# Windowed-attention block on Trainium2: TensorE's order of work regrouped by tile form

## The chip, the cores and the metric

The kernel runs on one core of a Trainium2 chip. The metric is the device time of one execution in microseconds. A core has TensorE (matrix products, with a separate weight load ahead of each), VectorE, ScalarE, GpSimd and a queue that issues the DMAs. In the profile they are PE, PEld (the weight loads), DVE, ACT, POOL and SP. Only TensorE writes sums into the eight banks of PSUM; VectorE and ScalarE copy them out.

A word on "tile form": an instruction uses 128 or 64 (or 32) rows of TensorE's array and 128 or 64 of its columns. The profile's lines show it: `64*100` is a product with 64 rows of input and 100 output columns, which takes the 64-row x 128-column form; `103*64` takes the 128x64 form, `64*64` the 64x64 form, `128*128` the whole array. Products in disjoint tiles of one form run side by side.

## The reference

The input x is (4, 64, 128, 128). It is normalised in 32 groups of two channels. With h = that normalised x:

```
qkv  = conv3x3_depthwise(einsum("bchw,oc->bohw", h, w_qkv) + b_qkv) + b_dw   # 192 channels
q, k, v = qkv in windows of 8 x 8 pixels, 4 heads of 16 channels
attn = softmax(q @ k.T * temperature)                # 16 x 16 per window and head
out  = attn @ v
gate = gelu(v @ w_mlp.T + b_mlp)                     # over the 64 pixels of a window
y    = x + einsum("bchw,oc->bohw", out * gate, w_proj) + b_proj
```

## The kernel before, in words

Two images lie side by side in the 128 partitions (image, channel). The picture is cut into bands of 16 rows; a band of an image pair is a chunk, 16 chunks in all. A chunk has 16 column groups and is worked in four steps, a = 0 to 3, of four column groups each; `STEPS` is 64, and step i has a = i % 4. While chunk n is in its attention steps, TensorE also makes the q, k, v of chunk n + 1 as filler (`fillers`): in steps a = 0 and 1 eight units of channel mix each (`mix_channels`, the product with w_qkv over 10 x 10 patches, line 674), in steps a = 2 and 3 three units of depthwise convolution each (`depthwise`, line 709). Filler units go alternately through two work buffers of two PSUM banks (`unit_ps`). A number in `units()` gives each unit its buffer; the semaphores `full` and `free` hand it to the engine that copies it out and back (line 326 on ScalarE, line 417 on VectorE). The order of `units()` has to be the order in which TensorE issues them.

The other four banks (`rest_ps`) belong to the attention steps. Two of them are `pair_ps`: the mixed output of `apply_probs` (line 787) in columns 0 to 255 of both, the transposed v of `turn_v` in the whole first bank and the projection (line 796) in the whole second. Two are `score_ps`: scores in columns 0 to 255 (line 747) and the gate product in the rest (line 763).

A step on TensorE is: `score(i)`, fillers, `gates` (in steps a = 1 and 3, for two steps together, written one in two places), `project(i - 1)`, `turn_v(i)` (line 773, four 128 x 128 transposes), fillers, `apply_probs(i)`, fillers. The tuple `cut` says how many fillers stand where. On VectorE a step is: `mix(i - 1)` (output times gate, line 503), `scores_up` (mask, maximum, subtraction; lines 511, 516, 518), `gate_up` (adds b_mlp, line 525), `residual(i - 1)` (line 552), `divide` (sum, reciprocal, product; lines 532 to 536), `turn` (transpose of the probabilities, line 543), one depthwise copy in step a = 2, `normalise` (line 488, patches two chunks ahead) in steps 2 and 3, and in the first chunks statistics of the second image pair (`look`, line 496). ScalarE has the copies of the fillers, `exponent` (line 341), `v_up` (the copy of the transposed v, line 347), `gelu` (line 351) and the table loads (lines 351 and 356). All orders are written out by hand; each engine runs its own in order and waits on semaphores. The chunk's first scores wait until the last two depthwise copies of the chunk are done (`qkv_of`).

## Time and profile before

| | |
|---|---|
| three runs, median | 679.08 us |
| lowest, highest | 677.62, 679.31 us |
| profiled execution, from first to last instruction | 680.0 us |
| TensorE busy in it | 625.8 us, 92% |
| weight loads busy | 549.1 us, 81% |
| VectorE busy | 511.6 us, 75% |
| ScalarE busy | 482.8 us, 71% |

The profiled execution has no other time of its own than its span. Busy time of TensorE counts an instruction until its result has drained, so a busy TensorE is not one at its peak: consecutive instructions overlap, and the time that a block of work takes is read from its start to the start of the next block.

### The profile page before, as it was taken

The numbers are of one execution on the slowest core, as the hardware profiler recorded it, in microseconds if no ns is written. First come the engines' busy times: TensorE is split into PE (matmuls) and PEld (weight loads), VectorE is DVE, ScalarE is ACT, GpSimd is POOL, SyncE is SP. The second block draws the span as 40 slices with busy tenths as digits, with TensorE's granted clock in tenths as the row PEclk, the third lists the DMA queues.
The fourth block names the chain that finished last, engine by engine and source line by source line (L and its number), as shares of the span: only waits on it lengthen the run. The fifth ranks groups of instructions, "written<-read, shape, count | busy, mean of one in ns | idle before, by whom it ended". The sixth has DMA issues, their size and how long they took to land.

```text
span 680.0 us, 32438 instructions
## 1 busy us (share of the span) xinstructions
PE 625.8 (92%) x15044; PEld 549.1 (81%) x15044; DVE 511.6 (75%) x790; ACT 482.8 (71%) x631; POOL 0.3 (0%) x5
## 2 busy tenths in 40 slices
PE   3788799999999999999999999999999999999954
PEld 2687698888989898888989898888989798888843
DVE  4872688887888888786878676786868676876684
ACT  3652678787877778786877778786877778786722
POOL 0000000000000000000000000000000000000000
PEclk9997899999999999999999999999999999999975
DMA  9872115335171714132050504132150504112022
GB/s 363 263 217 72 33 50 166 110 86 208 33 232 49 234 59 149 66 102 93 8 191 5 195 4 142 60 94 106 29 173 4 198 3 152 44 50 80 4 82 44
DMA packets 29240, 72.28 MB, mean 106 GB/s; under 512 B 9801, under 2 KB 16329, under 8 KB 24233
## 3 DMA queue, kind: packets, MB, share of 16 engines
q1 hardware_dynamic: 28674, 68.57, 31.0%
q8 instruction: 118, 1.93, 1.2%
q10 hardware_dynamic: 432, 1.65, 0.7%
q14 instruction: 16, 0.13, 0.1%
HBM read 53.44 MB, written 16.78 MB: 103 GB/s over the span
## 4 chain that ended last, share of the span: by engine, by line
PE 87%; ACT 5%; DVE 3%; issue 2%; DMA 1%; ACTq 0%; DVEq 0%
PE unit_ps L709 28%; PE unit_ps L674 26%; PE rest_ps L796 10%; PE rest_ps L787 6%; PE rest_ps L763 6%; PE rest_ps L747 6%; PE rest_ps L773 4%; ACT z L326 2%; DMA patches<-in_hot 1%; ACT dw L326 1%; PE rest_ps L643 1%; PE rest_ps L674 1%; PE unit_ps L636 0%; DVE scores L511 0%; DVE scores L536 0%
## 5 line engine op out<-in xcount | busy, mean ns | idle before, releaser
L326 ACT ACTIVATE z<-unit_ps 100x768 f32<-100x768 f32 x244 | 184.9, 808 | 60.1 <-PE unit_ps L674 60.1
L674 PE MATMUL unit_ps<-consts,patches 64*100 64x192 f32 x1984 | 195.0, 336 | 8.6 <-ACT z L326 6.6
L709 PE MATMUL unit_ps<-z,dw 103*64 103x64 f32 (+2 forms) x6144 | 194.3, 224 | 3.0 <-issue 1.7
L709 PEld LDWEIGHTS unit_ps<-z,dw 103*64 103x64 f32 (+2 forms) x6144 | 185.5, 139 | 10.7 <-issue 8.6
L674 PEld LDWEIGHTS unit_ps<-consts,patches 64*100 64x100 f32 x1984 | 153.6, 164 | 25.8 <-ACT z L326 11.2
L326 ACT ACTIVATE qkv<-unit_ps 128x1024 f32<-128x1024 f32 x78 | 79.1, 1014 | 31.5 <-PE unit_ps L709 31.4
L511 DVE TENSOR_TENSOR scores<-rest_ps,consts 128x512 f32<-128x512 f32 x64 | 44.1, 689 | 51.6 <-PE rest_ps L747 51.6
L503 DVE TENSOR_TENSOR gate<-rest_ps,gate 128x512 f32<-128x512 f32 x64 | 44.1, 689 | 47.5 <-PE rest_ps L787 44.6
L796 PE MATMUL rest_ps<-gate,consts 128*128 128x256 f32 x256 | 75.1, 417 | 1.1 <-DVE gate L503 1.0
L347 ACT ACTIVATE v_t<-rest_ps 128x512 f32<-128x512 f32 x64 | 38.2, 597 | 40.5 <-PE rest_ps L773 38.9
L341 ACT ACTIVATE scores<-scores 128x512 f32<-128x512 f32 x64 | 40.4, 631 | 33.2 <-DVE scores L518 31.6
L787 PE MATMUL rest_ps<-v_t,probs_t 64*64 64x64 f32 x2048 | 45.5, 228 | 10.5 <-DVE probs_t L543 10.1
L525 DVE TENSOR_TENSOR gate<-rest_ps,consts 128x512 f32<-128x512 f32 x64 | 44.0, 687 | 14.4 <-PE rest_ps L763 14.0
L796 PEld LDWEIGHTS rest_ps<-gate,consts 128*128 128x128 f32 x256 | 44.9, 195 | 11.9 <-issue 3.5
L747 PE MATMUL rest_ps<-qkv 64*64 64x64 f32 x2048 | 45.4, 227 | 9.0 <-issue 9.0
L787 PEld LDWEIGHTS rest_ps<-v_t,probs_t 64*64 64x64 f32 x2048 | 36.7, 137 | 20.9 <-issue 18.8
L747 PEld LDWEIGHTS rest_ps<-qkv 64*64 64x64 f32 x2048 | 37.9, 138 | 18.1 <-issue 18.1
L552 DVE SCALAR_TENSOR_TENSOR staged<-rest_ps,consts,staged 128x512 f32<-128x512 f32 x64 | 46.7, 729 | 7.5 <-PE rest_ps L796 7.5
L543 DVE STREAM_TRANSPOSE probs_t<-scores 128x512 f32<-128x512 f32 x64 | 45.5, 712 | 2.2
L763 PE MATMUL rest_ps<-consts,qkv 64*64 64x64 f32 x2048 | 45.6, 228 | 1.6 <-DVE scores L511 1.6
L763 PEld LDWEIGHTS rest_ps<-consts,qkv 64*64 64x64 f32 x2048 | 36.7, 138 | 12.3 <-issue 8.2
L518 DVE TENSOR_TENSOR scores<-scores,neg_max 128x512 f32<-128x512 f32 x64 | 44.3, 692 | 2.2
(55 smaller groups left out, 530.5 us busy)
## 6 DMA issues: line engine op xcount, KB each, us to landing
staged<-in_x SPq DMA_DIRECT2D x17, 1024.0 KB, 4.9
out_y<-staged SPq DMA_DIRECT2D x15, 1024.0 KB, 5.4
T<-in_x SPq DMA_DIRECT2D x12, 1152.0 KB, 6.7
seen<-in_x SPq DMA_DIRECT2D x32, 256.0 KB, 2.9
qkv<-in_x SPq DMA_DIRECT2D x6, 1024.0 KB, 13.9
T<-in_x SPq DMA_DIRECT2D x3, 1088.0 KB, 6.7
staged<-in_x SPq DMA_DIRECT2D x2, 512.0 KB, 22.9
out_y<-staged SPq DMA_DIRECT2D x4, 256.0 KB, 3.0
```

Source lines behind the costliest of these rows:

```text
L326: return nc.scalar.activation(to, of, ACT.Copy)
L503: nc.vector.tensor_tensor(held, pair_ps[:, :, 0:BATCH * HW], held, ALU.mult).then_inc(mixed_ready, 1)
L511: nc.vector.tensor_tensor(scores[:].rearrange("p (h g) d -> p h g d", h=2), score_ps[:, :, 0:BATCH * C].rearrange("p h (g d) -> p h g d", ...
L518: nc.vector.tensor_tensor(scores[:], scores[:], neg_max[:].unsqueeze(2).to_broadcast([P, WIDE, C]), ALU.add).then_inc(shifted, 1)
L543: nc.vector.transpose(probs_t[:].rearrange("p w d -> p (w d)"), scores[:].rearrange("p w d -> p (w d)")).then_inc(probs_t_ready, 1)
L552: nc.vector.scalar_tensor_tensor(to, proj_ps.rearrange("p (r c) -> p r c", r=BAND), b_proj, to, op0=ALU.add, op1=ALU.add).then_inc(out_rea ...
L674: last = nc.tensor.matmul(to[0:NPATCH, t, b * QKV:(b + 1) * QKV], patches[image, b, g], w1[image], start=True, stop=True)
L709: last = nc.tensor.matmul(to[h * HW:(h + 1) * HW, m // 8, m % 8 * NW:(m % 8 + 1) * NW], dw[0:used, c, :], z[0:used, c, :], start=True, sto ...
L747: last = nc.tensor.matmul(score_ps[pair, h, g * C:(g + 1) * C], q[rows, pair], k[rows, pair], start=True, stop=True)
L763: last = nc.tensor.matmul(gate_ps[side(b, h), b, g * HW:(g + 1) * HW], windows(j, g)[rows, 2, b * C:(b + 1) * C], mlp[rows], start=True, s ...
L787: last = nc.tensor.matmul(pair_ps[side(b, h), b, g * HW:(g + 1) * HW], probs_t[rows, h * BATCH + g, :], v_t[rows, at], start=True, stop=True)
L796: last = nc.tensor.matmul(proj_ps[:, b * 4 * HW:(b + 1) * 4 * HW], proj[:, b * P:(b + 1) * P], gate[:, i % GATES, b].rearrange("p g (r c) ...
```

## The change

TensorE's order is put together by tile form. `turn_v` uses two 64-row halves per column group instead of one 128 x 128 transpose and writes into a work buffer, as a unit of the ring (`turns_in`): steps 0 and 1 of a chunk (a = 0 and 1) make their own turn and that of the step two later, steps 2 and 3 make none. Its copy is a `v_up` on ScalarE for step i and one on VectorE for step i + 2; the v of steps 2 and 3 waits in its own places (`v_ts`, one of them in the space of `tap_w`). The projection is two 64-column halves per bank (`project`), or in steps after a = 3 and 0 two rounds of 64 rows (`project_half`). It writes columns 256 to 511 of both `pair_ps` banks. The gates of two steps stand behind each other ahead of `apply_probs` in steps 0 and 2; the even one writes where the projection does (`proj_ps`), the odd one beside the scores. `scores` of row half h and image b go to bank h ^ b. VectorE adds b_mlp to the two gates one step later than TensorE makes them: in step 1 ahead of `scores_up` and behind `v_up`, in step 3 behind `scores_up`. In step 3, ScalarE copies depthwise 4 and 5 out between the two GELUs.

```diff
+def turns_in(i):
+    return [("turn", j) for j in (i + 2, i)] if i % BATCHES < 2 else []
 def gates_in(i):
-    return (0, 1) if i == 0 else (i + 1, i + 2) if i % 2 and i + 2 < STEPS else ()
+    return [i + 2, i + 3] if i % 2 == 0 and i + 2 < STEPS else []
...
+        def v_up(engine, copy, i):
+            unit = ("turn", i)
+            used = i if i % BATCHES == 1 else i - 2 if i % BATCHES == 0 else i - 3
+            if used > 0:
+                engine.wait_ge(mix_done, used)
+            wait_full(engine, unit)
+            copy(v_ts[i % BATCHES].rearrange("p (h x) -> p h x", h=2),
+                 work[buffer(unit)][:, :, 0:BATCH * HW]).then_inc(free[buffer(unit)], 1)
...
                 for j in now:
                     gelu(j)
                     if more and a == 3 and j == now[0]:
                         evacuate_dw(act, copy, n, 4)
-                if more and a == 3:
-                    evacuate_dw(act, copy, n, 5)
+                        evacuate_dw(act, copy, n, 5)
...
+                now = gates_in(i - 1) if i else [0, 1]
+                if now and a == 1:
+                    gate_up(now[0])
                 scores_up(i)
-                now = gates_in(i)
+                if now and a != 1:
+                    gate_up(now[0])
+                for unit in turns_in(i)[:1]:
+                    v_up(dve, copy, unit[1])
                 if now:
-                    gate_up(now[0])
-                elif i:
+                    gate_up(now[1])
+                if i:
                     residual(i - 1)
                 divide(i)
                 turn(i)
...
             def turn_v(i):
-                if i:
-                    pe.wait_ge(mixed_ready, i)
+                unit = ("turn", i)
+                to = take(unit)
                 for g in range(BATCH):
-                    last = nc.tensor.transpose(pair_ps[:, 0, g * P:(g + 1) * P], windows(i, g)[:, 2], ident)
-                last.then_inc(v_t_done, 1)
+                    for h in range(2):
+                        rows = slice(h * HW, (h + 1) * HW)
+                        last = nc.tensor.transpose(to[:, h, g * HW:(g + 1) * HW], windows(i, g)[rows, 2],
+                                                   ident[rows, rows])
+                last.then_inc(full[buffer(unit)], 1)
...
+            def wait_gated(i):
+                pe.wait_ge(mixed_ready, i + 1)
+                for j in gates_in(i)[:1]:
+                    pe.wait_ge(gate_biased, j + 1)
             def project(i):
-                pe.wait_ge(mixed_ready, i + 1)
+                wait_gated(i)
                 for b in range(2):
-                    last = nc.tensor.matmul(proj_ps[:, b * 4 * HW:(b + 1) * 4 * HW], proj[:, b * P:(b + 1) * P],
-                                            gate[:, i % GATES, b].rearrange("p g (r c) -> p r g c", c=WS),
-                                            start=True, stop=True)
+                    for t in range(2):
+                        last = nc.tensor.matmul(proj_ps[t * C:(t + 1) * C, b],
+                                                proj[:, b * P + t * C:b * P + (t + 1) * C], gated(i, slice(0, P), b),
+                                                start=True, stop=True)
                 last.then_inc(proj_done, 1)
+            def project_half(i, second):
+                if second:
+                    pe.wait_ge(half_done, i // BATCHES * 2 + (i % BATCHES == BATCHES - 1) + 1)
+                else:
+                    wait_gated(i)
+                for b in range(2):
+                    rows = slice((b ^ second) * HW, (b ^ second) * HW + HW)
+                    last = nc.tensor.matmul(proj_ps[:, b], proj[rows, b * P:(b + 1) * P], gated(i, rows, b),
+                                            start=not second, stop=bool(second))
+                last.then_inc(proj_done if second else half_done, 1)
...
             for i in range(STEPS):
+                a, units_now, turns = i % BATCHES, fillers(i), turns_in(i)
...
                 score(i)
+                if not units_now:
                     project(i - 1)
+                    fill(turns)
+                elif a < 2:
+                    if i:
+                        fill(units_now[:1])
+                        project_half(i - 1, 0)
+                        fill(units_now[1:2])
+                    fill(turns[:1])
+                    if i:
+                        project_half(i - 1, 1)
+                    fill(turns[1:])
+                    fill(units_now[2:6])
+                elif a == 2:
+                    project(i - 1)
+                    fill(units_now)
+                else:
+                    fill(units_now[:1])
+                    project(i - 1)
+                    fill(units_now[1:])
+                for j in gates_in(i):
+                    gates(j, i)
                 apply_probs(i)
+                if a < 2:
+                    fill(units_now[6:])
             project(STEPS - 1)
```

## Rows read from the trace of the kernel before

**Rows 1.** The page, busy time, share of the span and instructions of each engine.
```profile
PE 625.8 (92%) x15044; PEld 549.1 (81%) x15044; DVE 511.6 (75%) x790; ACT 482.8 (71%) x631; POOL 0.3 (0%) x5
```
**Rows 2.** The page, chain of waits: shares of the span by engine, by line.
```profile
PE 87%; ACT 5%; DVE 3%; issue 2%; DMA 1%; ACTq 0%; DVEq 0%
PE unit_ps L709 28%; PE unit_ps L674 26%; PE rest_ps L796 10%; PE rest_ps L787 6%; PE rest_ps L763 6%; PE rest_ps L747 6%; PE rest_ps L773 4%; ACT z L326 2%; DMA patches<-in_hot 1%; ACT dw L326 1%; PE rest_ps L643 1%; PE rest_ps L674 1%; PE unit_ps L636 0%; DVE scores L511 0%; DVE scores L536 0%
```
**Rows 3.** Stretches (first, fifth, last chunk): length, busy of PE, PEld, DVE, ACT, POOL, clock.
```profile
66.68:109.60 42.92, 38.59 (x974) 33.77 (x973) 32.36 (x50) 31.39 (x42) 0.00 (x0) 0.92 0.12 33
223.79:261.79 38.00, 37.14 (x929) 32.61 (x929) 32.00 (x50) 29.43 (x40) 0.00 (x0) 1.00 0.41 132
643.73:680.03 36.30, 19.77 (x356) 15.55 (x356) 24.84 (x40) 10.01 (x15) 0.00 (x0) 0.68 0.26 59
```
**Rows 4.** Timeline of PE, sixth chunk: start us, us, instructions merged [idle before <- releaser].
```profile
261.79 0.77 PE L747 MATMUL rest_ps<-qkv 64*64 64x64 f32 x32 [0.60 <-issue]
262.49 1.55 PE L674 MATMUL unit_ps<-consts,patches 64*100 64x192 f32 x16
263.97 1.13 PE L796 MATMUL rest_ps<-gate,consts 128*128 128x256 f32 x4
264.93 0.60 PE L773 MATMUL rest_ps<-consts,qkv 128*128 128x128 f32 x4
265.46 1.55 PE L674 MATMUL unit_ps<-consts,patches 64*100 64x192 f32 x16
267.27 1.60 PE L674 MATMUL unit_ps<-consts,patches 64*100 64x192 f32 x16 [0.26 <-ACT z L326]
...
273.01 0.69 PE L763 MATMUL rest_ps<-consts,qkv 64*64 64x64 f32 x32
273.63 1.13 PE L796 MATMUL rest_ps<-gate,consts 128*128 128x256 f32 x4
...
282.93 5.82 PE L709 MATMUL unit_ps<-z,dw 103*64 103x64 f32 x192
288.68 0.69 PE L787 MATMUL rest_ps<-v_t,probs_t 64*64 64x64 f32 x32
289.20 0.65 PE L747 MATMUL rest_ps<-qkv 64*64 64x64 f32 x32
289.77 2.09 PE L709 MATMUL unit_ps<-z,dw 103*64 103x64 f32 x64
...
298.57 0.69 PE L787 MATMUL rest_ps<-v_t,probs_t 64*64 64x64 f32 x32
299.87 0.69 PE L747 MATMUL rest_ps<-qkv 64*64 64x64 f32 x32 [0.60 <-issue]
```
**Rows 5.** Timeline of PE in two narrow windows: the first records of a block.
```profile
262.49 0.57 PE L674 MATMUL unit_ps<-consts,patches 64*100 64x192 f32 x4
...
263.97 0.70 PE L796 MATMUL rest_ps<-gate,consts 128*128 128x256 f32 x2
```
**Rows 6.** Timeline of ACT, sixth chunk.
```profile
263.43 1.51 ACT L326 ACTIVATE z<-unit_ps 100x768 f32<-100x768 f32 x2 [0.23 <-PE unit_ps L674]
264.83 0.63 ACT L341 ACTIVATE scores<-scores 128x512 f32<-128x512 f32 x1
265.57 0.60 ACT L347 ACTIVATE v_t<-rest_ps 128x512 f32<-128x512 f32 x1
266.41 1.51 ACT L326 ACTIVATE z<-unit_ps 100x768 f32<-100x768 f32 x2 [0.24 <-PE unit_ps L674]
...
299.79 1.28 ACT L356 ACT_TABLE_LOAD   x1
```
**Rows 7.** Timeline of DVE, sixth chunk.
```profile
287.00 1.22 DVE L417 COPY qkv<-unit_ps 128x1024 f32<-128x1024 f32 x1 [0.20 <-PE unit_ps L709]
...
289.48 0.69 DVE L503 TENSOR_TENSOR gate<-rest_ps,gate 128x512 f32<-128x512 f32 x1
...
291.52 0.69 DVE L518 TENSOR_TENSOR scores<-scores,neg_max 128x512 f32<-128x512 f32 x1
```

More of the change, by code:

```diff
@@ L66, in units @@
     for i in range(STEPS):
-        order += fillers(i)
+        fill, turns = fillers(i), turns_in(i)
+        if i == 0:
+            order += fill[:2] + turns + fill[2:]
+        else:
+            order += [*fill[:1], *fill[1:2], *turns, *fill[2:]]
     return {name: at for at, name in enumerate(order)}
@@ L236, in evacuate_dw @@
             if n > 1:
-                engine.wait_ge(v_t_done, (n - 1) * BATCHES)
+                wait_full(engine, ("turn", (n - 1) * BATCHES - 3))
             wait_full(engine, unit)
@@ L379, in _ @@
                     exponent(i)
-                    v_up(i)
+                    v_up(act, copy, i)
                     if more:
@@ L718, in fill @@
                         depthwise(*unit[1:])
+                    elif unit[0] == "turn":
+                        turn_v(unit[1])
                     elif unit[0] == "mean":
@@ L739, in score @@
                     pe.wait_ge(masked, i)
-                    pe.wait_ge(gate_biased, max(j for m in range(i) for j in gates_in(m)) + 1)
                 for g in range(BATCH):
@@ L746, in score @@
                             rows = slice(h * HW, (h + 1) * HW)
-                            last = nc.tensor.matmul(score_ps[pair, h, g * C:(g + 1) * C], q[rows, pair], k[rows, pair],
+                            last = nc.tensor.matmul(score_ps[pair, h ^ b, g * C:(g + 1) * C], q[rows, pair], k[rows, pair],
                                                     start=True, stop=True)
@@ L762, in gates @@
                             rows = slice(h * HW, (h + 1) * HW)
-                            last = nc.tensor.matmul(gate_ps[side(b, h), b, g * HW:(g + 1) * HW],
+                            last = nc.tensor.matmul(gate_ps[j % 2][side(b, h), b, g * HW:(g + 1) * HW],
                                                     windows(j, g)[rows, 2, b * C:(b + 1) * C], mlp[rows],
@@ L781, in apply_probs @@
                     pe.wait_ge(out_ready, i)
+                for j in gates_in(i)[:1]:
+                    pe.wait_ge(gate_done, j + 1)
                 for g in range(BATCH):
                     for h in range(2):
-                        at = slice((2 * g + h) * HW, (2 * g + h + 1) * HW)
+                        at = slice((h * BATCH + g) * HW, (h * BATCH + g + 1) * HW)
                         for b in range(2):
                             rows = slice(b * C, (b + 1) * C)
-                            last = nc.tensor.matmul(pair_ps[side(b, h), b, g * HW:(g + 1) * HW],
-                                                    probs_t[rows, h * BATCH + g, :], v_t[rows, at],
+                            last = nc.tensor.matmul(mix_ps[side(b, h), b, g * HW:(g + 1) * HW],
+                                                    probs_t[rows, (h ^ b) * BATCH + g, :], v_ts[i % BATCHES][rows, at],
@@ L789, in apply_probs, with gated @@
                                                     start=True, stop=True)
                 last.then_inc(mix_done, 1)
+            def gated(i, rows, b):
+                return gate[rows, i % GATES, b].rearrange("p g (r c) -> p r g c", c=WS)
+            def wait_gated(i):
+                pe.wait_ge(mixed_ready, i + 1)
+                for j in gates_in(i)[:1]:
+                    pe.wait_ge(gate_biased, j + 1)
             def project(i):
-                pe.wait_ge(mixed_ready, i + 1)
+                wait_gated(i)
```

64 lines of the change are left out of this document (23 added, 41 removed).

## The prediction

> **What bounds the kernel now.** I read the busy shares first: TensorE is busy 92% of the span, VectorE 75%, ScalarE 71% [rows 1]. The chain of waits says the same: 87% of it is TensorE, in the depthwise, channel-mix and projection products [rows 2]. The stretch view shows the repeated unit: one chunk of four steps takes 38.00 us with TensorE busy 37.14 of it [rows 3]. Fifteen such chunks make the kernel, so each 0.1 us in a chunk is 1.5 us. The last question is what TensorE's time consists of, and for that I read its order of work line by line, in the chunk behind that one [rows 4, 5].
>
> A change of tile form has a price. Two matmul blocks of the 64x64 form behind each other (apply, then scores) take 289.77 - 288.68 = 1.09 us; a lone block of it takes 273.63 - 273.01 = 0.62. So the seam costs 1.25 - 1.09 = 0.16 if the form changes and nothing if it doesn't [rows 4]. Channel mix (64 rows x 128 columns): 16 records last 1.55, 4 last 0.57, so two records take 0.163 and a unit of eight 0.65; a block of two units takes 1.48 to the next block, 0.18 over its 1.30 [rows 4, 5]. Depthwise (128x64): 3 units take 288.68 - 282.93 = 5.75; a unit is 1.87 (192 records last 5.82, 64 last 2.09, the difference over two), and 5.75 less 3 x 1.87 leaves 0.15 [rows 4]. The 128x128 block (projection and turn): 265.46 - 263.97 = 1.49, of which the projection's four records are 4 x 0.215 and the four transposes 4 x 0.109 (0.60 less one duration of 0.27, over 3); 0.19 remains [rows 4, 5].
>
> With these the four steps of a chunk before, by their tile-form blocks (5, 9, 4 and 7), are 8.48, 9.91, 8.39 and 9.88 us, together 36.66; the trace has 38.00. The 1.34 between are two waits: 0.56 where four mix units stand in a row (a pair takes 267.27 - 265.46 = 1.81 instead of 1.30, because the buffer comes free by ScalarE), and 0.79 ahead of the chunk's first scores, which wait for ScalarE's last depthwise copy (299.87 - 298.57 = 1.30 where 0.52 is work) [rows 4, 6].
>
> **The change, part by part.**
> Blocks. After, step 0 of a chunk is scores | mix, half projection, mix, turn, half, turn, 4 mix | gates, gates, apply | 2 mix. Step 1 is the same without gates. Step 2 is scores | projection, 3 depthwise | gates, gates, apply, and then step 3's scores with no seam; step 3 is 1 depthwise, projection, 2 depthwise | apply, and the next scores with no seam. That is 12 blocks instead of 25.
>
> Work inside the blocks. The projection keeps its columns: two 64-column tiles side by side, or two halves of 64 rows side by side, four rounds of 256 columns each way, 0.86. The trace has no 64-row transpose. Its lower bound is 4 rounds at a 64x64 block's pace (0.52 / 8 = 0.065), 0.26 a step; its upper bound, if the two row halves don't run side by side, is 8 x 0.109 = 0.87. I take 4 x 0.109 = 0.44, today's price: each weight load still has 128 columns, and mix shows two row halves running as a pair. The Trainium skill (TensorE: Matmul & The Clock Gate, section LDWEIGHTS) prices a load by its columns alone; an estimate by its figure would be 4 x 128 / 1.2 ns = 0.43, which no run shows yet for this form. Pure work is then step 0: 0.63 + (0.18 + 6 x 0.65 + 0.86 + 0.87) + 1.56 + 1.48 = 9.47; step 1: 0.63 + 5.81 + 0.63 + 1.48 = 8.54; step 2: 0.63 + (0.15 + 0.86 + 5.60) + 1.45 = 8.69; step 3: 0.58 + 6.61 + 0.52 = 7.71. Sum 34.41, which is 2.25 less than 36.66. (Two turns each stand in steps 0 and 1, none in 2 and 3.)
>
> New waits, the ring. The turn leaves its own bank and goes through the two work buffers, so steps 0 and 1 send ten units through the ring instead of eight. From the start of a mix unit to ScalarE's copy is 263.43 - 262.49 = 0.94, and from that copy's start to TensorE's restart in the buffer 267.27 - 266.41 = 0.86; a restarted mix unit needs 0.73, since its first weight load (0.08) isn't hidden, and a turn 0.11 more for the same reason [rows 4, 6]. I walk step 0 from the start of its scores. Mix 0 runs 0.63 to 1.36. ScalarE is not free: the second GELU (0.63, as the exponent over as many columns) now stands behind the last depthwise copy, and the table load (1.28) behind that [rows 6], so its copy of mix 0 starts at 1.9 and not at 1.57. Half projection and mix 1 end at 2.44; the first turn wants mix 0's buffer, free at 2.76, and ends at 3.30; half projection to 3.73; second turn to 4.17. VectorE copies the first turn from 3.44 to 4.13 (0.69, as for another 512 columns out of PSUM [rows 7]), so mix 2 starts at 4.19. ScalarE copies the second from 4.31 to 4.91 (0.60 [rows 6]); mix 3 starts at 4.96. Mix 4 and 5 follow 1.81 behind 2 and 3, to 7.50. Then seam and gates, gates, apply to 9.16, two mixes to 10.63: 1.16 of waits, where step 0 had 0.56. Step 1 by the same walk: the second turn waits for mix 1's copy (3.60 instead of 3.31, plus 0.11), mixes 2 to 5 start at 4.14, 4.93, 5.94, 6.74; the step takes 9.67, so 1.13 of waits where it had none. Added: 1.73.
>
> New wait, step 3. The projection there must also see gate j biased, j being the first gate of step 2, since both lie in one bank. VectorE does that behind step 2's product with the gate and step 3's three passes over the scores. From the scores' start, the product starts at 289.48 - 289.20 = 0.28 and the third pass ends at 292.21 - 289.20 = 3.01 [rows 7]; the bias add ends at 3.65, TensorE sees it at 3.7. It comes to the projection at 0.58 + 1.92 = 2.49. It waits 1.21 and restarts with 0.05: 1.26. Behind it in TensorE's queue stand two depthwise units, whose last copy holds back the next chunk's scores, so nothing gives it back. (Step 1 has the same wait, but there VectorE adds the bias ahead of the scores, and two mixes cover it.)
>
> What stays. The 0.79 ahead of the chunk's scores is unchanged: its copy still follows the last depthwise unit. In step 2 the gates wait for VectorE's copy of depthwise 1, there at 7.2 after 5.99 + 1.22 [rows 7], when TensorE comes at 7.24: 0.02. The softmax chain ends before apply in each step (7.1 against 9.1 in the tightest but one, level in step 3). The DMAs keep order and slack.
>
> Sum for a chunk: -2.25 + 1.73 + 1.26 + 0.02 = +0.76, 38.76 instead of 38.00. Fourteen chunks: +10.6. The first chunk is a case of its own (42.9 us, granted clock 0.92 on average, so partly at the lower level [rows 3]); I take it as even: two gate blocks more ahead of its first scores, and less waiting behind its first GELUs, which the longer step 0 covers in part. The last chunk is a chain VectorE - ScalarE - TensorE (36.3 us from its start to the end [rows 3]); two more 0.69 passes ahead of the softmax's end, partly in the exponent's shadow, less one moved behind, give +0.6. Together +11.2: the profiled span goes from 680.0 to 691.2, and as the median of the runs shown (679.08) lies 0.95 under that span, 690 us.
>
> A page of the Trainium skill speaks against the regrouping: PSUM, section PSUM bank collisions raise a hardware error, has it that different row tiles can't use one bank at the same time. In the scores each bank is now written from both row halves (bank h ^ b), which would make their rounds run one after the other. But the gates already write that way (both row halves into bank b, other partitions), and their block takes 0.62 to the next block [rows 4], as a scores block does; if the rule did bite, scores would take 0.47 more a step, about +28 us in all. I give it 2 in 100.
>
> **Rivals.**
> A, faster: the ring hides its waits. ScalarE is busy only 29.4 of 38 us a chunk and VectorE 32.0 [rows 3], which speaks for it; against it, the four-unit run waits already [rows 4]. Then -2.25 + 1.26 = -0.99 a chunk, 15 chunks, -15: 664 us. Between it and the forecast all values can be had; the sign turns where the new waits of a chunk fall under 2.25 us. If the step 3 wait alone is missing, it is 690 - 19 = 671. Chance 0.23 for what ends faster.
> B, much slower: a turn's two row halves run one after the other, +0.44 for each turn, all on the path as the ring is the path there: +1.75 a chunk, +26, 716 us. Against it, the mix's pairs; for it, that no transpose of this form is in the trace. Chance 0.05.
> C, the bank rule above: 718 us, 0.02.
> D, a transpose next to matmuls of its own form counts as a change of form: 8 seams of 0.17 a chunk, +20, 710 us. The 128x128 transposes stand behind the 128x128 projection without any seam (264.93 - 263.97 = 0.97 for 4 x 0.215 and the block's head [rows 4, 5]), so 0.02.
>
> **Numbers.** The forecast, slower by 8 to 16 us, has 0.68. 0.3% (2 us) is what a measurement here tells from no change. Faster by more than that 0.23, within it 0.05, slower 0.72. The range reaches from 671 (no wait in step 3) to 700 (half-way to D): some 2 in 10 lie outside, most of them A's far end, B and C. The likeliest case's own range is 684 to 697.
>
> **What would show it.** Chunks of 38.8 us, TensorE's blocks in a chunk 12, its busy time lower by some 2 us; projection in step 3 starting 1.2 us after the depthwise unit ends, released by VectorE's bias add; mix units in steps 0 and 1 released by ScalarE and VectorE copies; a turn of 0.44 us. Wrong if chunks are under 38 us, or if the turns take 0.87 or 0.26.

## The result, and the profile after

The changed kernel takes 695.64 us, the median of 4 runs (694.88 to 697.28); the kernel before takes 678.35 beside it on the same chip (4 runs, 677.38 to 679.31). The ratio is 1.0265, with a 95% interval of 1.0245 to 1.0285. The profiled execution has a span of 693.6 us where before it has 680.0, so the profiles show 13.6 of the 17.3 us between the medians. Most of the other 3.7 is the choice of trace: every recorded execution takes 1.7 to 1.9 us more than its span, so the profiled execution of before is one of about 681.8 us, 3.4 over the median of its kernel, with 13.7 us at the low granted clock from 59.6 on. Like for like the growth is about 17 us. Three executions at a far lower granted clock, one each of two kernels below and one of the kernel before beside them, are left out of the medians and ratios.

The page after: busy shares, the chain of waits by engine, and the queue that brings instructions. They answer to [rows 1, 2].

```profile
span 693.6 us, 33456 instructions
PE 612.5 (88%) x15556; PEld 522.6 (75%) x15556; DVE 525.4 (76%) x822; ACT 470.5 (68%) x599; POOL 0.3 (0%) x5
q8 instruction: 122, 2.00, 1.1%
PE 69%; ACT 16%; DVE 8%; issue 6%; DMA 1%; ACTq 0%; DVEq 0%
```

TensorE works 13.3 us less and the kernel is 13.6 us longer: waits have taken the place of work. The chain tells which: ScalarE 5% to 16%, VectorE 3% to 8%, "issue" 2% to 6%.

The second and the last chunk after, in the stretch view (columns as in [rows 3]):

```profile
107.89:146.25 38.36, 36.43 (x960) 31.10 (x961) 32.78 (x52) 28.69 (x38) 0.00 (x0) 1.00 0.39 130
655.16:693.65 38.49, 18.57 (x392) 12.56 (x392) 26.18 (x42) 9.41 (x14) 0.00 (x0) 0.63 0.24 56
```

Step 0 of the ninth chunk and the head of its step 1, TensorE, answering to [rows 4]:

```profile
383.66 0.69 PE L762 MATMUL rest_ps<-qkv 64*64 64x64 f32 x32 [0.40 <-issue]
384.29 0.90 PE L688 MATMUL unit_ps<-consts,patches 64*100 64x192 f32 x8
385.02 0.60 PE L842 MATMUL rest_ps<-gate,consts 64*128 64x256 f32 x4
385.45 0.82 PE L688 MATMUL unit_ps<-consts,patches 64*100 64x192 f32 x8
386.35 0.46 PE L793 MATMUL unit_ps<-consts,qkv 64*128 64x64 f32 x8
386.64 0.65 PE L842 MATMUL rest_ps<-gate,consts 64*128 64x256 f32 x4
387.18 0.46 PE L793 MATMUL unit_ps<-consts,qkv 64*128 64x64 f32 x8
387.66 1.63 PE L688 MATMUL unit_ps<-consts,patches 64*100 64x192 f32 x16
389.47 1.62 PE L688 MATMUL unit_ps<-consts,patches 64*100 64x192 f32 x16 [0.18 <-ACT z L347]
391.02 1.16 PE L781 MATMUL rest_ps<-consts,qkv 64*64 64x64 f32 x64
392.01 0.66 PE L810 MATMUL rest_ps<-v_t,probs_t 64*64 64x64 f32 x32
392.60 1.55 PE L688 MATMUL unit_ps<-consts,patches 64*100 64x192 f32 x16
394.08 0.69 PE L762 MATMUL rest_ps<-qkv 64*64 64x64 f32 x32
```

The order is the one I walked through. Step 0 takes 394.08 - 383.66 = 10.42. The turn (L793) at 386.35 gives way to the next block at 386.64: 0.29, not 0.44. The head of the row at 385.45 to that at 386.35 is 0.90 where a unit's work is 0.65; most of the waits are as small as that and bear no mark, since they are shorter than the modelled duration of the records ahead of them. Scores, whose two row halves now share banks, still take 384.29 - 383.66 = 0.63 to the next block.

Step 3 of the same chunk, TensorE and VectorE:

```profile
412.49 0.68 PE L762 MATMUL rest_ps<-qkv 64*64 64x64 f32 x32
412.76 0.69 DVE L515 TENSOR_TENSOR gate<-rest_ps,gate 128x512 f32<-128x512 f32 x1 [1.10 <-PE rest_ps L810]
413.10 1.85 PE L723 MATMUL unit_ps<-z,dw 103*64 103x64 f32 x56
414.81 0.69 DVE L530 TENSOR_TENSOR scores<-scores,neg_max 128x512 f32<-128x512 f32 x1
415.41 0.68 DVE L537 TENSOR_TENSOR gate<-rest_ps,consts 128x512 f32<-128x512 f32 x1
415.45 0.45 PE L723 MATMUL unit_ps<-z,dw 103*64 103x64 f32 x8 [0.50 <-issue]
416.24 1.08 PE L829 MATMUL rest_ps<-gate,consts 128*64 128x256 f32 x8 [0.34 <-DVE gate L537]
417.13 3.93 PE L723 MATMUL unit_ps<-z,dw 103*64 103x64 f32 x128
```

The bias add ends 416.09 - 412.49 = 3.60 behind the scores' start and the projection starts at 3.75 (forecast 3.65 and 3.7). But the depthwise unit ahead of it has a hole of its own: 56 of its 64 products, then 0.50 of "issue", a wait for nothing that the profile shows, then the last 8. Here that hole lies in the shadow of the wait for the bias. Elsewhere it doesn't, as in the chunk before:

```profile
373.88 0.67 PE L762 MATMUL rest_ps<-qkv 64*64 64x64 f32 x32
374.48 0.27 PE L723 MATMUL unit_ps<-z,dw 109*64 109x64 f32 x1
375.63 2.08 PE L723 MATMUL unit_ps<-z,dw 109*64 109x64 f32 x63 [0.88 <-issue]
```

These holes were not in my prediction. I numbered all TensorE records of the trace (a record is one weight load, product or semaphore instruction). TensorE's stops with no semaphore behind them lie ahead of one position, the 193rd of a 256; a hole is from here on what lies over 0.2 us between the starts of two records there. In the 14 chunks from the second to the last but one, the kernel after has 18 at that position, 14.4 us together, and the kernel before 1, 0.3 us. Both kernels have a longer one earlier, while the first chunk's depthwise units are made; before:

```profile
58.12 1.09 PE L709 MATMUL unit_ps<-z,dw 106*64 106x64 f32 x30 [1.68 <-issue]
```

In the 14 chunks the holes go with the pace: of the places where the last 256 records took less than 3.05 us, after has 16, of which 12 have a hole (10.1 us); of the 90 slower ones 6 have one (4.3 us). Before, the fastest 256 take 3.05. What makes them fast is the run gates, gates, apply, scores, all 64x64: 256 records in about 1.9 us.

### The profile page after: what moved, and what is told of

Its sections match the earlier page's. It is cut to its first block, busy times and chain, and to the rows that moved or that the text cites. A ratio compares the mean times of both kernels' runs of the same rounds, so it can differ in the third digit from the quotient of the medians.

```text
span 693.6 us, 33456 instructions
## 1 busy us (share of the span) xinstructions
PE 612.5 (88%) x15556; PEld 522.6 (75%) x15556; DVE 525.4 (76%) x822; ACT 470.5 (68%) x599; POOL 0.3 (0%) x5
## 4 chain that ended last, share of the span: by engine, by line
PE 69%; ACT 16%; DVE 8%; issue 6%; DMA 1%; ACTq 0%; DVEq 0%
PE unit_ps L723 23%; PE unit_ps L688 21%; ACT z L347 7%; PE rest_ps L781 5%; PE rest_ps L829 5%; PE rest_ps L810 4%; PE rest_ps L762 4%; PE unit_ps L793 3%; ACT L371 2%; PE rest_ps L842 2%; ACT qkv L347 2%; DVE neg_max L528 2%; DVE scores L523 1%; DMA patches<-in_hot 1%; ACT dw L347 1%
## 5 line engine op out<-in xcount | busy, mean ns | idle before, releaser
L347 ACT ACTIVATE z<-unit_ps 100x768 f32<-100x768 f32 x244 | 191.8, 808 | 72.8 <-PE unit_ps L688 70.8
L688 PE MATMUL unit_ps<-consts,patches 64*100 64x192 f32 x1984 | 207.1, 338 | 13.1 <-ACT z L347 4.4
L723 PEld LDWEIGHTS unit_ps<-z,dw 103*64 103x64 f32 (+2 forms) x6144 | 187.9, 138 | 17.3 <-issue 12.9
L723 PE MATMUL unit_ps<-z,dw 103*64 103x64 f32 (+2 forms) x6144 | 190.9, 222 | 11.2 <-issue 9.9
L688 PEld LDWEIGHTS unit_ps<-consts,patches 64*100 64x100 f32 x1984 | 150.0, 163 | 45.3 <-ACT z L347 20.0
L829 PE MATMUL rest_ps<-gate,consts 128*64 128x256 f32 x280 | 41.3, 417 | 9.1 <-DVE gate L537 8.2
L548 DVE TENSOR_TENSOR scores<-scores,inv_total 128x512 f32<-128x512 f32 x64 | 44.3, 692 | 2.2
L528 DVE TENSOR_REDUCE neg_max<-scores 128x8 f32<-128x512 f32 x64 | 43.9, 686 | 2.2
L544 DVE TENSOR_REDUCE total<-scores 128x8 f32<-128x512 f32 x64 | 43.5, 679 | 0.6
L810 PE MATMUL rest_ps<-v_t,probs_t 64*64 64x64 f32 x1536 | 34.5, 226 | 9.1 <-DVE probs_t L555 7.7
```

Of the source, the lines that this page charges most:

```text
L347: return nc.scalar.activation(to, of, ACT.Copy)
L528: nc.vector.tensor_reduce(neg_max[:], scores[:], AX_X, ALU.max, negate=True).then_inc(max_ready, 1)
L688: last = nc.tensor.matmul(to[0:NPATCH, t, b * QKV:(b + 1) * QKV], patches[image, b, g], w1[image], start=True, stop=True)
L723: last = nc.tensor.matmul(to[h * HW:(h + 1) * HW, m // 8, m % 8 * NW:(m % 8 + 1) * NW], dw[0:used, c, :], z[0:used, c, :], start=True, sto ...
L810: last = nc.tensor.matmul(mix_ps[side(b, h), b, g * HW:(g + 1) * HW], probs_t[rows, (h ^ b) * BATCH + g, :], v_ts[i % BATCHES][rows, at], ...
L829: last = nc.tensor.matmul(proj_ps[t * C:(t + 1) * C, b], proj[:, b * P + t * C:b * P + (t + 1) * C], gated(i, slice(0, P), b), start=True, ...
```

## The experiments

In the table "undisturbed" is the shortest that a step takes in chunks 1 to 13, which holds no hole; "holes" are those of over 0.2 us at that 193rd record in the 14 chunks. The ratio is to the kernel before, run beside each.

| kernel | undisturbed steps 0 to 3 | chunk | 14 chunks in the trace | holes | median, us | ratio, 95% |
|---|---|---|---|---|---|---|
| before | 9.04 9.91 8.39 10.67 | 38.00 | 534.1 | 1, 0.3 us | 678.35 | 1 |
| after | 10.42 9.46 8.69 9.78 | 38.35 | 547.3 | 18, 14.4 | 695.64 | 1.0265 |
| after, gates between | 10.23 9.46 8.69 9.78 | 38.16 | 544.1 | 21, 16.0 | 695.69 | 1.0252 (1.0216 to 1.0288) |
| after, late copy behind GELUs | 10.41 9.46 8.69 9.78 | 38.34 | 549.5 | 18, 16.6 | 698.63 | 1.0314 (1.0255 to 1.0374) |
| after, all three | 10.23 9.46 8.69 9.55 | 37.93 | 544.1 | 26, 20.2 | 699.14 | 1.0315 (1.0248 to 1.0382) |
| after, bias first and gates between | 10.23 9.46 8.69 9.08 | 37.46 | 542.1 | 23, 19.1 | 692.04 | 1.0196 (1.0150 to 1.0241) |
| the same, mix ahead of scores | 9.70 9.46 8.69 9.32 | 37.18 | 544.0 | 24, 20.3 | 693.36 | 1.0215 (1.0196 to 1.0233) |
| before, projection in 64 columns | 9.14 10.01 8.49 10.77 | 38.41 | 540.8 | 5, 1.6 | 685.32 | 1.0097 (1.0052 to 1.0142) |
| before, dense run | 9.04 9.91 8.39 11.67 | 39.00 | 557.1 | 13, 9.3 | 706.49 | 1.0423 (1.0398 to 1.0447) |
| before, mix ahead of scores | 8.43 9.91 8.39 10.82 | 37.55 | 528.1 | 2, 0.7 | 671.37 | 0.9899 (0.9881 to 0.9918) |

**One new wait at a time.** The first takes the wait for the gate's bias out of step 3: VectorE adds the bias to the first gate ahead of its passes over the scores, in all steps but the very first.

```diff
-                if now and a == 1:
+                if now and i:
                     gate_up(now[0])
                 scores_up(i)
-                if now and a != 1:
+                if now and not i:
                     gate_up(now[0])
```

> The changed kernel, with one edit: in step 3 VectorE adds the bias to the first gate ahead of its three passes over the scores, as it does in step 1 already. Theory (the projection in step 3 stands waiting for that bias add, 1.2 us a chunk, and nothing gives it back): the bias add ends 1.6 us after the step's scores start instead of 3.65, TensorE comes at 2.49, so the wait goes; the softmax of that step is 0.6 later, which apply only just feels. Step 3 goes from 9.8 to 8.7 or 8.8 us, 15 chunks, -15 us: 680 us. Rival 1: the wait only changes its name, since apply in step 3 hangs on VectorE's chain (level with TensorE before): under 0.3 us a chunk, 691 or more. Rival 2: instruction supply. The changed kernel's trace has TensorE stalls with no semaphore behind them, at records 256 apart, and in step 3 some lie in the shadow of the projection's wait; without the wait they would show, about 0.4 us a chunk: 686.

Measured 692.32 us (three runs, 688.48 to 694.44), ratio 1.019 (1.0132 to 1.0248), where 680 was expected. That is 3 us under the changed kernel instead of 15, nearest in time to rival 1, 691 or more. Its one trace is of the execution that is left out, and isn't read here; a later kernel shows the same edit, and there step 3 does get shorter.

The second lets ScalarE copy depthwise unit 5 behind both GELUs and not between them.

```diff
                         evacuate_dw(act, copy, n, 4)
-                        evacuate_dw(act, copy, n, 5)
+                if more and a == 3:
+                    evacuate_dw(act, copy, n, 5)
```

> The changed kernel, with one edit: in step 3 ScalarE copies the last depthwise unit out behind both GELUs, as before the change, not between them. Theory (the ring in step 0 waits for ScalarE, which comes 0.6 us late because a GELU and the table load stand behind that copy): the second GELU fits into ScalarE's idle time ahead of the copy, ScalarE is free 1.4 instead of 2.0 us after the chunk's scores start; the first turn of step 0 then waits for nothing, 0.25 to 0.4 us a chunk, -4 to -6 us: 690 us. Rival: the ring in step 0 is set by what follows (exponent, copy of the turn, four copies of mixes), and nothing moves: 695.6.

No step moved by over 0.01: the first turn of step 0 isn't held by ScalarE's late start on mix 0. The rival was right, and that edit is worth nothing by itself (698.63 us, 3 above the changed kernel, with 2.2 us more in holes). Together with the bias first it costs: step 3 takes 9.55 with both and 9.08 with the bias first alone.

The third puts step 0's gates between its fourth and fifth mix, so that 64x64 work fills the ring's wait.

```diff
-                    fill(units_now[2:6])
+                    fill(units_now[2:4])
+                    if a == 0:
+                        for j in gates_in(i):
+                            gates(j, i)
+                    fill(units_now[4:6])
```

> The changed kernel, with one edit: in step 0 the two gate blocks stand between the third and fourth of the six mixes that follow each other, not ahead of apply. It costs two seams of form (0.34 us). Theory (ring waits are time in which other work is free): the waits ahead of mixes 4 and 5, 0.45 us, are covered, and 64x64 work is spread, so that fewer records come in a short time: about -0.2 us a chunk from the ring and up to -0.2 from instruction supply, 690 to 693 us. Rival (seams are what counts): +0.34 us a chunk, 700 us.

Step 0 fell by 0.19, as expected of the ring, and the 14 chunks of the trace by 3.1, though the holes grew by 1.6. The median didn't fall: in this trace the time up to the second chunk is 110.7 us against 107.9, with more of it at a low granted clock.

> The changed kernel with the three edits together: bias first in step 3, the depthwise copy behind both GELUs, gates between the mixes in step 0. If the three waits are separate, the gains add: -1.05 - 0.35 - 0.2 us a chunk, about -24 us in 15 chunks: 672 us, under the kernel before. If they hand one wait on to the next, or the stalls without a semaphore come out of their shadow, 678 to 684 us.

The miss was large: 699.14 (three runs, 697.19 to 704.35). The waits did go (an undisturbed chunk of 37.93), and the 14 chunks still took 544.1. Holes went from 14.4 to 20.2 us, and the start of the second chunk lay at 114.0. That made the holes the question.

**Are the holes tied to a place in the program, or to a count?** Sixteen one-column products more ahead of the first chunk, 64 records, leave every wait between engines as it is and shift the count under the same code.

```diff
             idle_products(24)
+            for _ in range(16):
+                nc.tensor.matmul(rest_ps[:, 0, 0:1], group_mean, w1[:, 0:1], start=True, stop=True)
```

> The changed kernel with 16 one-column products more ahead of the first group mean, 64 TensorE records and no other edit; they cost up to 4 us once. In the changed kernel's trace, every TensorE stall over 0.2 us with no semaphore behind it stands at record 193 of a block of 256 (weight loads and products counted together), and nearly all of them where the last 256 records took less than 3.05 us; such blocks are where the 64x64 run (gates, gates, apply, scores) of steps 2 and 3 falls into one. Theory (the instruction stream is supplied in blocks of 256, and is late behind such a run): the stalls stay at record 193 of a block, so they move 64 records earlier in the program: the blocks of step 3 that end short after the run are then those of the chunks with index 1, 3, 5, 6, 8, 10 and 12, 0.3 to 1.9 us after the scores' start, and the stalls at 2.0 to 3.2 us of the changed kernel are gone. Rival (they belong to a place in the program, a buffer or a bank): they stay at the same products and stand at record 1 of a block.

There were 18 holes of over 0.2 us in the 14 chunks, again all at the 193rd of 256; those of step 3 stand in all seven chunks listed, and in a few more. One at 2.4 us into a step 3 was not expected. So it is the count. (706.69 us, a single run, whose first scores came 7 us later than after's; its time says nothing of the shift.)

**What does a turn cost in the ring?** This kernel leaves out the turns of V for steps 2 and 3 (those steps use the V of step 1, so the output is not attention's). VectorE's two copies of those turns go too, and all steps share one place for V.

```diff
-    return [("turn", j) for j in (i + 2, i)] if i % BATCHES < 2 else []
+    return [("turn", i)] if i % BATCHES < 2 else []
...
-                for unit in turns_in(i)[:1]:
-                    v_up(dve, copy, unit[1])
```

> The changed kernel without the turns of steps 2 and 3: those steps use the transposed v of step 1, so that their output is not the reference's. Steps 0 and 1 send nine units through the ring instead of ten, TensorE has 0.6 us less work in a chunk, VectorE two copies of 0.69 less. Theory (what sets steps 0 and 1 is ScalarE's chain: copy of mix 1, exponent, copy of the near turn, then the mixes two by two; the far turn stands in its shadow): steps 0 and 1 stay within 0.1 us of the changed kernel's 10.42 and 9.47, and the time at 694 to 696 us. Rival (TensorE's time adds up, the far turns are on the path with their 0.3 us and their wait): -0.3 to -0.6 us in each of the two steps, 15 chunks: 678 to 686 us.

Undisturbed, steps 0 and 1 took 10.20 and 9.25, 0.21 or 0.22 less each: one turn of 0.29 gone, of which the ring takes 0.08 back. That lies between the theory (0.1) and the rival (0.3 to 0.6) and is no more than the turn itself. 689.25 us, ratio 1.0168 (1.0115 to 1.0221).

**What is a seam worth?** A seam is a change of tile form between two blocks. The kernel before, with the projection in two halves of 64 output columns: one seam more a step, the same columns.

```diff
-                    last = nc.tensor.matmul(proj_ps[:, b * 4 * HW:...], proj[:, b * P:(b + 1) * P],
-                                            gate[:, i % GATES, b]..., start=True, stop=True)
+                    for t in range(2):
+                        last = nc.tensor.matmul(proj_ps[t * C:(t + 1) * C, b * 4 * HW:...],
+                                                proj[:, b * P + t * C:b * P + (t + 1) * C],
+                                                gate[:, i % GATES, b]..., start=True, stop=True)
```

> The kernel before, with one edit: each projection as two 64-column halves (128x64 form) in place of the 128x128 form. The columns streamed stay the same; in its place beside the 128x128 transposes it makes one seam of form more in each step. Theory (a seam costs 0.15 to 0.2 us wherever TensorE is the bound): +0.16 a step, 60 steps, +10 us, 686 to 690 us. Rival (the gaps between blocks are the unhidden weight load alone, not a drain): the shorter weight load of 64 columns gives 0.05 back and the seam costs 0.05 to 0.1, +0 to +3 us: 679 to 682.

```profile
300.90 1.55 PE L674 MATMUL unit_ps<-consts,patches 64*100 64x192 f32 x16
302.38 1.08 PE L797 MATMUL rest_ps<-gate,consts 128*64 128x256 f32 x8
303.39 0.66 PE L773 MATMUL rest_ps<-consts,qkv 128*128 128x128 f32 x4
303.98 1.55 PE L674 MATMUL unit_ps<-consts,patches 64*100 64x192 f32 x16
```

Projection and turn take 303.98 - 302.38 = 1.60 where they took 1.49 [rows 4], and every step is 0.10 longer. The first weight load of a block isn't hidden behind a seam; from it to the next load it is 0.055 us in this 64-column projection and 0.108 in the 128-column one of before. So the seam alone costs about 0.16, of which the shorter first load gave 0.05 back. Seams are real, at 0.10 to 0.16 each. The time, 685.32, lies between the forecasts of the theory and of the rival.

**Do the undisturbed steps say where the time goes?** Bias first and gates between together, and then the first mix ahead of the scores as well.

> The changed kernel with the bias first in step 3 and the gates between the mixes in step 0, ScalarE's order as changed. With all three edits step 3 stood at 9.55 us, since the second GELU delayed the last depthwise copy; without that it should be 9.1. A chunk is then 10.23 + 9.47 + 8.69 + 9.1 = 37.5 us where no stall falls, against 38.35 of the changed kernel and 38.00 before. Theory (this sum, plus 0.6 us a chunk of supply stalls that now have no shadow in step 3): 684 to 689 us. Rival (step 3 only hands its wait on): 9.5 or more, 690 to 695 us.

> The changed kernel with the bias first in step 3 and the gates between the mixes in step 0 (692.0 us), and with the first mix of step 0 ahead of the scores, in the time in which the scores wait for the last depthwise copy. It takes the 64x64 run of apply and scores apart and costs two seams. Theory: the mix waits 0.3 us for VectorE's patches and fills the rest of the 0.7 us wait, -0.3 us a chunk, and somewhat fewer supply stalls: 684 to 689 us. Rival (the patches come so late that the scores start later by the whole mix): +0.3 us a chunk, 696 us.

The undisturbed chunk of the first, 37.46, is what was expected to 0.04, and 0.54 under before's 38.00. If the 14 chunks were undisturbed it would beat the kernel before by 7 us. It is nearly 14 us slower (692.04, where 684 to 689 was expected): the 14 chunks are 542.1, 17.7 above 14 x 37.46. Step 3, TensorE:

```profile
409.39 0.68 PE L762 MATMUL rest_ps<-qkv 64*64 64x64 f32 x32
409.99 1.85 PE L723 MATMUL unit_ps<-z,dw 103*64 103x64 f32 x56
412.34 0.45 PE L723 MATMUL unit_ps<-z,dw 103*64 103x64 f32 x8 [0.50 <-issue]
412.62 1.03 PE L829 MATMUL rest_ps<-gate,consts 128*64 128x256 f32 x8
```

The projection follows the depthwise unit without the wait for VectorE (compare L829 above), and the hole, which that wait used to cover, now shows: the projection starts 3.23 after the scores, where it starts after 2.57 in a step 3 without a hole (chunk 13, the first being 0). The second has yet shorter steps (37.18) and yet more holes, and is no faster (693.36, again 684 to 689 expected). Removing waits paid less than it saved. That waits had spread the records out, and the holes grew as they went, fits these runs; the next one tests it.

**Is a dense run enough?** The kernel before, with 32 one-column 64x64 products ahead of step 3's scores (128 records), and nothing else.

```diff
+                for g in (*range(BATCH), *range(BATCH)) if i % BATCHES == 3 else ():
+                    ...
+                            nc.tensor.matmul(score_ps[pair, h, 0:1], q[rows, pair], k[rows, pair][:, 0:1],
+                                             start=True, stop=True)
```

> The kernel before, with one edit: in step 3, ahead of the scores, 32 one-column products of the scores' own operands and form (64x64), whose results the scores overwrite. They make 128 TensorE records more, between apply and the scores: a run of 256 records of 64x64 form, as the changed kernel has it at this place, and no seam. By weight loads alone they cost 8 rounds x 2 records x 0.055 us = 0.9 us a chunk. Theory (instruction supply in blocks of 256 is late behind such a run): besides, step 3 gets stalls at record 193 of a block, which the kernel before has once at most, in about half of the chunks and of up to 1.5 us; step 3 then varies between chunks; 15 x (0.9 + 0.4) = +20 us: 694 to 702 us. Rival (the stalls of the changed kernel come from something else in it): every chunk has the same step 3, 11.5 us, and no such stalls: 690 to 692 us.

```profile
174.71 0.83 PE L747 MATMUL rest_ps<-qkv 64*64 64x1 f32 x47
175.73 0.41 PE L747 MATMUL rest_ps<-qkv 64*64 64x1 f32 x17 [0.19 <-issue]
175.99 0.67 PE L755 MATMUL rest_ps<-qkv 64*64 64x64 f32 x32
176.59 2.09 PE L709 MATMUL unit_ps<-z,dw 103*64 103x64 f32 x64
178.61 0.46 PE L771 MATMUL rest_ps<-consts,qkv 64*64 64x64 f32 x14
180.40 0.50 PE L771 MATMUL rest_ps<-consts,qkv 64*64 64x64 f32 x18 [1.33 <-issue]
```

Steps 0 to 2 are to the hundredth as before. Step 3 takes between 11.67 and 13.57, where it took 10.67 in 12 of the 14 chunks of before. The 14 chunks are 1.64 longer each: 1.00 for the products at least, and 9.3 / 14 = 0.66 for 13 holes, all at the 193rd of 256. The rival, the same step 3 in every chunk and no holes, is out. So records packed into the order of before make the holes without any of the change's other parts. That is the shown part of the cause. The time, 706.49, is above the 694 to 702 of the theory.

**A version that beats both.** The prediction's other wait of before, 0.79 us ahead of a chunk's first scores [rows 4], is filled with work that waits for nothing: the kernel before with the first mix of step 0 ahead of the scores.

```diff
+                early = i and i % BATCHES == 0 and bool(units_now)
+                if early:
+                    fill(units_now[:1])
                 if i % BATCHES == 0:
                     qkv_of(i // BATCHES)
...
-                    fill(units_now[:cut[0]])
+                    fill(units_now[early:cut[0]])
```

> The kernel before, with one edit: in step 0 of a chunk the first of the two mixes that followed the scores stands ahead of them. Theory: the scores wait 0.79 us there for the last depthwise copy; the mix (0.65, with 0.18 of seams) fills that, the patches are there in time (VectorE's pass ends 0.2 us ahead of apply), and no long 64x64 run arises, so no supply stalls: the block structure gives -0.45 us a chunk, -6 us: 671 to 674 us, faster than both kernels. Rival (ScalarE is late for the first mix's copy by its table load, 1.5 us, and the ring hands the wait on to the run of four mixes): -0.1 us a chunk or nothing, 676 to 678 us.

```profile
409.12 0.69 PE L787 MATMUL rest_ps<-v_t,probs_t 64*64 64x64 f32 x32
409.74 0.90 PE L674 MATMUL unit_ps<-consts,patches 64*100 64x192 f32 x8
410.57 0.69 PE L747 MATMUL rest_ps<-qkv 64*64 64x64 f32 x32
411.20 0.90 PE L674 MATMUL unit_ps<-consts,patches 64*100 64x192 f32 x8
```

671.37 us (6 runs, 670.34 to 674.26), 1% faster than before, and clear of noise (0.9881 to 0.9918). From apply to scores it is 1.45 instead of 1.30, with a mix unit inside; an undisturbed chunk is 0.45 shorter, and with only 2 holes (0.7 us) that is also about what the time shows: 15 x 0.45 = 6.8 us, beside 7.0 between the medians.

## Why the prediction was right, and where it was not

The time was forecast as 690, the medians say 695.6: the right side, within the range, 5.6 us short. In the profiles it is 13.6 of growth against 11.2. That this is close is partly luck: the chunk's own growth was forecast twice too large, and a term of 8.2 us was missing. Of the 5.6 us, some 3 come from neither: the forecast took 0.95 off the span to reach the median, as the profile of before stood that much above its median, while after's median stands 2.0 above its span.

**Blocks and seams: right.** The timelines show 12 blocks, and step 2, which the change only relieves, takes 8.69 (forecast 8.70 or 8.71). The price of a seam was confirmed by adding one.

**The ring in steps 0 and 1: the mechanism right, the turn mis-sized.** Forecast 10.63 and 9.67, measured 10.42 and 9.46. The failing number is the turn, 0.29 instead of 0.44: not today's price for four transposes but close to the lower bound of 0.26, which I had also named as a sign of being wrong. Four rounds are 0.074 each, near a 64x64 block's 0.065. I took the upper of two near rows because the loads keep their 128 columns. The Trainium skill (TensorE: Matmul & The Clock Gate, section LDWEIGHTS) prices loads by columns alone, whatever the rows, which gave the same 0.43. The trace disagrees: in the turn, as in the half projection, a load of 64 rows x 128 columns takes 0.055 us from its start to the next load's, where one of 128 rows x 128 columns took 0.108 before. Two turns are 0.30 shorter than forecast and the step 0.21; the rest is waits that the copies set.

**The projection's wait for the bias: right.** 3.60 and 3.75 measured for 3.65 and 3.7, and step 3 is 9.78 (forecast 7.71 + 1.26 + 0.79 = 9.76). Its removal gave back 0.70 of the 1.26 (9.78 to 9.08), so "nothing gives it back" was too strong. The trace with the bias first shows where most of the rest went, in chunk 13:

```profile
608.97 1.92 ACT L347 ACTIVATE qkv<-unit_ps 128x1024 f32<-128x1024 f32 x2
609.38 0.88 PE L810 MATMUL rest_ps<-tap_w,probs_t 64*64 64x64 f32 x32
610.99 0.69 PE L762 MATMUL rest_ps<-qkv 64*64 64x64 f32 x32 [0.73 <-issue]
```

From apply to the next scores it is 1.61 where after has 1.09 in the same chunk (615.29 to 616.38): the scores wait for ScalarE's last depthwise copies, which end at 610.89.

**The chunk.** +0.35 measured where the steps summed to +0.76; 14 times that is +5.0, not +10.6.

**TensorE busy: wrong.** I said some 2 us less a chunk; it is 0.71 (37.14 to 36.43). Busy time runs to the modelled end of each record, so a wait of 0.2 between two blocks counts as busy. The work went down by more, and the busy row can't show it.

**The missing term: the supply of TensorE's instructions.** The 14 chunks of the trace grew by 13.1, of which 5.0 is structure and 8.2 is not in any undisturbed step. The holes there sum to 14.4 us, part of them in the shadow of other waits, as in step 3 above. The forecast had no term for it. The signs of it in the trace of before are the hole of 1.9 us at 58 us and one of 0.31 in a 256 of 3.10 us; I had read "issue" only as the 2% of the chain [rows 2]. The shown part is that holes come at a fixed count of 256 records, and with dense records. That they are waits for a block of instructions is inferred. For it: the instruction queue of the page moves 122 packets of 2.00 MB, 16 KB each, and the trace has 31402 TensorE records, 122.7 times 256 (before: 118 packets and 118.7 times). In the DMA records of the trace such a packet lands 1.26 to 1.54 us ahead of TensorE's restart in 16 of the 18 holes, and nowhere in the 14 chunks of after does a 193rd record start sooner than 1.26 us behind a landing. The Trainium skill (Runtime: NRT & Kernel Launch, section Instruction fetch mechanics) has instructions come in 16 KiB blocks of 256 by a queue that the sequencer drives, which fits. The Trainium skill also has the crossing "mostly hidden"; that holds in the 14 chunks of before, though not at 58 us, and not here, where it costs up to 2.1 us a time.

The DMA records also tell of the six holes behind 256 records that took over 3.05 us. Two are no supply holes: the one of 0.26 us ends with ScalarE's copy, and at the one of 0.25 the packet had landed 5.3 us earlier. In the other four (0.44 to 1.31 us) the packet started late, 2.0 to 3.6 us behind the previous 193rd record where 1.0 is the median, and in that time the DMA engines were busy with data, by a share of 0.76 to 1.05. The longest of these delays, columns as in [rows 3] with the DMA share and GB/s at the end:

```profile
151.06:154.64 3.58, 3.39 (x94) 2.68 (x96) 3.17 (x6) 3.07 (x4) 0.00 (x0) 1.00 1.05 323
```

The hole at 58 us is of the same kind in both kernels (the packet starts 3.1 and 3.2 us behind the previous 193rd record, with a share of 0.98 and 0.92). So a hole comes from dense records or from a late packet. That the data transfers are what delays the packet is read from the traces, and no run tests it.

**The last chunk: mis-sized.** +2.2 (36.30 to 38.49) for +0.6, of which 1.50 is its second step. VectorE there, after:

```profile
665.25 0.69 DVE L530 TENSOR_TENSOR scores<-scores,neg_max 128x512 f32<-128x512 f32 x1
666.35 0.69 DVE L429 COPY tap_w<-unit_ps 128x512 f32<-128x512 f32 x1 [0.41 <-PE unit_ps L793]
666.96 0.68 DVE L537 TENSOR_TENSOR gate<-rest_ps,consts 128x512 f32<-128x512 f32 x1
667.55 0.74 DVE L564 SCALAR_TENSOR_TENSOR staged<-rest_ps,consts,staged 128x512 f32<-128x512 f32 x1
668.21 0.68 DVE L544 TENSOR_REDUCE total<-scores 128x8 f32<-128x512 f32 x1
```

The exponent lasts from 665.97 to 666.60. Three passes and a wait for the turn stand between it and the total, which starts 1.6 after the exponent's end. I counted passes and took the exponent to cover part; the turn's copy waits itself, and the projection's pass moved ahead of the total too.

**The first chunk** was taken as even and came out 1.7 us shorter up to its end (109.60 to 107.89), with the stretches of low granted clock in other places: 13.7 us from 59.6 before, 3.4 from 78.4 after. That is the one traced execution of before: the three traces of edited versions of it end their first chunk at 107.87 to 108.00. Traces of edited versions of after have it at 108.0 to 115.3, so this term varies by more than it was forecast to.

**Rivals.** A (the ring hides its waits) fell: the waits are there. B and C fell on the rows of the turn and of the scores. D fell: two turns stand between mix and projection without 0.17 at each side.

**Open.** Why 4 of the 16 fast places of after have no hole was not traced, and no run changes how instructions are supplied. What sets the clock's low stretches in the first chunk is open too.

## What to carry to other kernels

Before packing small products behind each other, number TensorE's records in the trace and see how long 256 of them take: where the kernel of this case came under about 3 us for 256, holes of 0.2 to 2 us came in 12 of 16 places, and removing further waits uncovered them. Look also for idle TensorE with no releaser where data transfers fill the DMA engines. Seams between tile forms cost 0.10 to 0.16 us each here, less than one wait for a buffer shared with another engine, so count the waits that a regrouping makes before the seams that it takes. The gain of this case came from moving an independent unit into a wait: the first mix ahead of the scores, 7 us.

## What the runs showed of the hardware

- TensorE stops at one fixed place in each 256 of its records: 18 holes, 14.4 us, in 14 chunks of after, with runs of 64x64 fp32 products (two weight loads and two products each) at 256 records in about 1.9 us. An instruction packet of 16 KB lands 1.26 to 1.54 us ahead of the restart in 16 of them.
- Such a packet can start 2 to 3.6 us behind the previous 193rd record, where 1.0 is the median, while data transfers keep the DMA engines busy: ahead of the hole of 1.9 us at 58 us in both kernels, and of four of the 18 in after.
- Transposes in fp32 of 64 rows x 128 columns, two row halves beside each other, take 0.29 us for four pairs; four of 128 x 128 took 4 x 0.109 [rows 4]. The weight load of 64 rows x 128 columns takes 0.055, that of 128 x 128 takes 0.108.
- Two row halves that write one bank at the same time, on different output partitions, run at full pace: 0.63 us for a scores block, as before.
- A change of form between 64x64, 64x128, 128x64 and 128x128 blocks costs 0.15 to 0.19 us, of which the first weight load, not hidden, is 0.055 to 0.108.
